# Four cross-attention layers on one core: the leftover keys' score products placed singly among the key groups of a sweep

## The reference, cut to what matters

```python
qh = (q @ Wq + bq).reshape(B, Lq, H, D).transpose(0, 2, 1, 3)
kh = (k @ Wk + bk).reshape(B, k.shape[1], H, D).transpose(0, 2, 1, 3)
vh = (v @ Wv + bv).reshape(B, v.shape[1], H, D).transpose(0, 2, 1, 3)
att = jnp.einsum('bhqd,bhkd->bhqk', qh, kh) * scale
att = jax.nn.softmax(att, axis=-1)
y = jnp.einsum('bhqk,bhkd->bhqd', att, vh)
...
x = x + jnp.tanh(g_xattn[0]) * _L0_xattn_ref(_layernorm(x), ctx_1024, ctx_1024, ...)
x = x + jnp.tanh(g_ffn[0]) * _L0_ffn_ref(_layernorm(x), ...)
```

## Time and profile before

| | us |
|---|---|
| median of 3 runs (3147.51 to 3158.24) | 3156.18 |
| the profiled execution's own time | 3158.26 |
| span of its trace | 3156.5 |
| PE busy in the span | 3041.5 (96%) |
| ACT busy | 2547.7 (81%) |
| DVE busy | 438.2 (14%) |
| POOL busy | 196.5 (6%) |

### The profile page before, as it was taken

The page is one execution under the profiler, slowest core; times in us unless marked ns, Lnnn a source line. Parts: engine busy times, 40 slices in busy tenths (PEclk is TensorE's granted clock), DMA queues, the critical chain, the costliest instruction groups (busy, mean ns, idle before and its releaser), DMA issues.

```text
span 3156.5 us, 56669 instructions
## 1 busy us (share of the span) xinstructions
PE 3041.5 (96%) x18432; PEld 1131.8 (36%) x18432; DVE 438.2 (14%) x1290; ACT 2547.7 (81%) x2960; POOL 196.5 (6%) x715
## 2 busy tenths in 40 slices
PE   6799999999989989999999999899899999999999
PEld 3432222322233532322332323666522222322256
DVE  3600000100012420000110001644300000100012
ACT  3489999999963269999999998332299999999963
POOL 2000000000000000000000000200000000000000
PEclk9989999999989989999999999999999999999999
DMA  6811111111140011111111113110011111111110
GB/s 190 235 34 37 37 37 36 37 38 37 37 110 0 1 33 37 38 37 37 60 43 38 38 37 93 38 56 1 1 35 37 37 37 43 57 38 37 37 39 7
DMA packets 147561, 146.31 MB, mean 46 GB/s; under 512 B 17512, under 2 KB 100956, under 8 KB 147436
## 3 DMA queue, kind: packets, MB, share of 16 engines
q1 hardware_dynamic: 141552, 142.57, 14.6%
q10 hardware_dynamic: 5884, 2.08, 0.3%
HBM read 115.21 MB, written 29.57 MB: 46 GB/s over the span
## 4 chain that ended last, share of the span: by engine, by line
PE 92%; DVE 4%; issue 1%; SPq 1%; POOL 1%; ACT 1%; DMA 1%; ACTq 0%; DVEq 0%; POOLq 0%
PE PS L2124 39%; PE PS L2143 32%; PE PS L740 5%; PE PS L725 5%; PE PS L727 2%; PE PS L1036 2%; PE PS L1022 1%; SPq L1511 1%; PE PS L1961 0%; PE PS L1023 0%; PE PS L1071 0%; PE PS L1971 0%; PE PS L2038 0%; PE PS L2104 0%; PE PS L2110 0%
## 5 line engine op out<-in xcount | busy, mean ns | idle before, releaser
L1897 ACT ACTIVATE probs<-PS 128x1024 f32<-128x1024 f32 x2496 | 2276.3, 1417 | 26.0 <-PE PS L2143 22.3
L2124 PE MATMUL PS<-probs,vr 128*32 128x512 f32 (+1 forms) x9984 | 1328.3, 604 | 1.9 <-DVE accs L2363 1.9
L2143 PE MATMUL PS<-qs,kr 35*128 35x512 f32 (+2 forms) x4992 | 1109.0, 492 | 6.6 <-ACT probs L1897 3.5
L2143 PEld LDWEIGHTS PS<-qs,kr 35*128 35x128 f32 x4992 | 459.9, 184 | 1278.0 <-ACT probs L1897 1101.1
L763 ACT ACTIVATE probs<-PS 128x512 f32<-128x512 f32 x192 | 114.5, 597 | 272.4 <-PE PS L725 144.3
L1731 POOL COPY vr<-vs 128x72 f32 (+1 forms) x624 | 157.7, 253 | 2793.0 <-PE PS L2124 2453.4
L2124 PEld LDWEIGHTS PS<-probs,vr 128*32 128x32 f32 x9984 | 197.4, 108 | 321.7 <-issue 213.9
L2363 DVE COPY accs<-PS 128x512 f32<-128x512 f32 x12 | 8.3, 692 | 1301.2 <-PE PS L2110 1301.2
L740 PEld LDWEIGHTS PS<-wide,probs 128*128 128x128 f32 x1280 | 151.5, 194 | 17.5 <-issue 16.7
L740 PE MATMUL PS<-wide,probs 128*128 128x128 f32 x1280 | 153.8, 277 | 0.5 <-DVE kf L798 0.5
L2361 DVE TENSOR_TENSOR PS<-PS,stair 128x256 f32<-128x256 f32 x64 | 25.3, 430 | 659.5 <-PE PS L2143 659.5
(11 more groups left out here) (299 smaller groups left out, 1152.5 us busy)
## 6 DMA issues: line engine op xcount, KB each, us to landing
kr<-key_pieces SPq DMA_DIRECT2D x1248, 64.0 KB
key_pieces<-kparts SPq DMA_DIRECT2D x36, 288.0 KB, 4.5
kr<-mask_strips SPq DMA_DIRECT2D x624, 4.0 KB
key_pieces<-probs SPq DMA_DIRECT2D x32, 288.0 KB, 4.8
vs<-values SPq DMA_DIRECT2D x2, 3672.0 KB, 16.9
values<-v_next SPq DMA_DIRECT2D x9, 432.0 KB, 5.5
values<-probs SPq DMA_DIRECT2D x8, 432.0 KB, 5.2
accs<-in_ctx SPq DMA_DIRECT2D x12, 192.0 KB, 4.3
```

The source lines that it names most:

```text
L1897: sc.activation(prob[n % RING][:, :, q0:], PS[:, bank:bank + 2, q0:], ACT.Exp, scale=SCALE).then_inc(p_ready, 1)
L2124: last = te.matmul(PS[32 * j:32 * j + 32, 7, q0:], vr[s.buf(c)][:, at_v:at_v + 32], prob[(n + j // 2) % RING][:, j % 2, q0:], start=fresh, ...
L2143: last = te.matmul(o, kr[b][own, p, :], qs[own, T8 // 2 * s.hh + p, 512 * s.qh + q0:512 * s.qh + 512], start=True, stop=True)
```

## The change

The four score products of a sweep's leftover keys are no longer one block at the joint behind it. Each stands alone behind a `values` call: in the second to fourth sweep of an attention in chunks 1 and 2 of that same sweep, in the first sweep in chunks 48 and 49. The value product of the second to fourth sweep moves into chunk 48 of its own sweep; that of the first sweep stays at the joint behind it. On ScalarE `exps_left` of the second to fourth sweep comes after that sweep's third chunk. TensorE's early transposes get a wait for the third sweep's `left_done` (bank 6), and DVE's copy of the accumulator now waits for the sweep's last `values` (`pv_done`) beside `left_used`.

```diff
--- before.py
+++ after.py
@@ -399,6 +399,8 @@
 
             if pair == 0:
                 pe.wait_ge(acc_ev, NSW * a + 2 * h + 2)
+                if h == 0:
+                    pe.wait_ge(left_done, NSW * a + 3)
             elif h == 0:
                 pe.wait_ge(at_rd, NT * a + 2)
             for j in range(2):
@@ -1906,8 +1908,10 @@
                     for c in range(TC):
                         for p in range(4):
                             exps(c, p)
-                            if prev and (c, p) == (0, 1):
+                            if s.w % NSW == 1 and (c, p) == (0, 1):
                                 exps_left(prev)
+                    if prev:
+                        exps_left(s)
                     with act.Fori(1, EXP_ROUND) as i:
                         for c in range(TC):
                             for p in range(4):
@@ -1921,8 +1925,6 @@
                     for c in range(ROUNDS_S * TC, s.n):
                         for p in range(4):
                             exps(c, p, q0=s.seen(c))
-                    if s.w % NSW == NSW - 1:
-                        exps_left(s)
                 between_act(act, a)
 
 
@@ -2093,16 +2095,18 @@
                 pe.wait_ge(qc_act, QU // 2 * (a + 1))
                 pe.wait_ge(qc_dve, QU // 2 * (a + 1))
 
-                def left_scores(s):
-
-                    if s.w % NSW == 0:
-                        pe.wait_ge(left_in, LEFT_IN * (a + 1))
-                    if s.w:
-                        pe.wait_ge(left_done, s.w)
-                    for tt in range(T8 // 2):
-                        t8 = T8 // 2 * s.hh + tt
-                        last = te.matmul(PS[:, 6, :], k_left[:, P * t8:P * t8 + P], qs[:, t8, 512 * s.qh:512 * s.qh + 512], start=(tt == 0), stop=(tt == T8 // 2 - 1))
-                    last.then_inc(left_ready, 1)
+                def left_scores(s, tt):
+
+                    if tt == 0:
+                        if s.w % NSW == 0:
+                            pe.wait_ge(left_in, LEFT_IN * (a + 1))
+                        if s.w:
+                            pe.wait_ge(left_done, s.w)
+                    t8 = T8 // 2 * s.hh + tt
+                    last = te.matmul(PS[:, 6, :], k_left[:, P * t8:P * t8 + P], qs[:, t8, 512 * s.qh:512 * s.qh + 512],
+                                     start=(tt == 0), stop=True, skip_group_check=True)
+                    if tt == T8 // 2 - 1:
+                        last.then_inc(left_ready, 1)
 
                 def left_values(s):
 
@@ -2146,15 +2150,17 @@
                     scores(0, 0)
                     if prev:
                         values(prev, prev.n - 1, 0)
-                        left_scores(prev)
                     scores(0, 1)
                     if prev:
                         values(prev, prev.n - 1, 1)
-                        left_values(prev)
+                        if prev.w % NSW == 0:
+                            left_values(prev)
                     for c in range(1, TC):
                         for g in range(2):
                             scores(c, g)
                             values(s, c - 1, g)
+                            if prev:
+                                left_scores(s, 2 * (c - 1) + g)
                     if s.w % NSW == 2:
                         for i in range(1, ROUNDS_S):
                             for c in range(TC):
@@ -2172,11 +2178,13 @@
                         for g in range(2):
                             scores(c, g)
                             values(s, c - 1, g)
+                            if prev is None and c < ROUNDS_S * TC + 2:
+                                left_scores(s, 2 * (c - ROUNDS_S * TC) + g)
+                        if prev and c == ROUNDS_S * TC:
+                            left_values(s)
                     if s.w % NSW == NSW - 1:
-                        left_scores(s)
                         for g in range(2):
                             values(s, s.n - 1, g)
-                        left_values(s)
 
                 between_pe(pe, a)
 
@@ -2360,6 +2368,7 @@
                             dve.wait_ge(s_ready, n + 1)
                             v.tensor_tensor(diagonal, diagonal, stair[:, :].unsqueeze(1).to_broadcast([P, 2, P]), ALU.add).then_inc(s_cut, 1)
                     dve.wait_ge(left_used, s.w + 1)
+                    dve.wait_ge(pv_done, s.quads + 2 * s.n)
                     v.tensor_copy(accs[:, s.hh, 512 * s.qh:512 * s.qh + 512], PS[:, 7, :]).then_inc(acc_ev, 1)
                     if s.w == NSW + 2:
                         scale_dve(dve, 0)
```

## The result

The change makes the kernel **slower by 0.5%**: median 3174.64 us over 20 executions against 3156.72 over 20; ratio 1.0052, 95% interval 1.0034 to 1.0069. One execution of each is some 2,100 us longer than the others; it counts in these medians (without it they are 3173.99 and 3156.26) but not in the ratio nor in what follows, where 19 of the changed kernel lie from 3153.19 to 3183.43 and 19 of the kernel before from 3147.05 to 3161.11. The forecast was 3157.5 with 3146 to 3165 as range, so the time lies outside it.

What follows compares the result with a forecast made beforehand. ScalarE was taken to set a sweep's pace, TensorE having 0.17 us to spare per step. The terms -6.7 + 3.7 + 8.2 + 1.5 - 5.4 gave +1.3 us, a median of 3157.5, range 3146 to 3165.

Steps and rivals of the forecast that it cites:

- rival D: TensorE's clock falls to 1.2 GHz, exponentials take 1.33 us each for 48 steps of two: +40, 3197 us; chance 0.01.
- item 1: Old losses at the joints between sweeps go: 6 x 1.0 and, in the second attention, 3 x 0.2; -6.7 us.
- batch rule: Skill rule that matmuls should go back to back in batches; by it dealing the products out is the wrong direction.
- Item 2: Value product of sweeps 1 to 3 moves into chunk 48: 9 x 0.41, +3.7 us.
- The single product: A lone score product between `values` and scores pays both edges, its weights not loaded ahead: 0.43 us.
- drain: Skill rule that a change of tiling mode drains TensorE; it spoke against the change, with 36 more such changes.
- rival B: Single products cost a quarter of the block, 0.285 us, weights loaded behind `values`: -4.4, 3151.8 us; chance 0.2.
- C: A drain on both sides of single products costs more than the block's edges show; at 0.8 us each, 3171; chance 0.09.
- Item 3: ScalarE time lost to single products in the sweeps and behind the joints, all three attentions: +8.2 us.
- the cover: Delay of a step's scores that ScalarE absorbs without loss: 0.64 us taken, 0.55 by a second reading.
- Item 5: Attention ends come earlier, the block and value product no longer behind the last exponential: 2 x 1.73 + 1.95, -5.4 us.
- Rival A: Everything hides: cover over 1.05 us, singles nearly free, -10.6, 3145.6 us; chance 0.07.

Runs made afterwards that it cites:

- b2_fill: The whole change, plus four extra score products as a block at joints 1 to 2 and 2 to 3 of the second attention; median 3158.74 us.
- a1_again: The changed kernel run again, unaltered; median 3164.44 us, ratio to the kernel before 1.0026 to 1.0066.
- a2_block: The change, with each sweep's four score products as one block (chunk 1 of sweeps 1 to 3, chunk 48 of sweep 0); median 3160.37 us.
- a4_outer: The change in the first and third attention only, the second as before; median 3158.06 us, ratio 0.9998 to 1.0020.
- d4_midspin: The change in the second attention only, plus four extra full-height products in chunk 1 behind joints 1 to 2 and 2 to 3; median 3163.65 us.
- c3_one: The change in the second attention only, with four extra products at joint 1 to 2 and nothing at joint 2 to 3; median 3160.90 us.
- c1_wait: The change in first and third attention only, TensorE awaiting the accumulator copy before chunk 1's scores at joints 1 to 2 and 2 to 3; median 3157.61 us.

## Why the prediction was wrong

- **What failed is the weighing of rival D, and item 1 behind it.** D was set at 0.01 because "with early work dealt between steps from 545 to 615 the clock stayed at 1.00". That row answers another question. It shows that work added between steps does no harm, and b2_fill agrees; the clock falls from what item 1 took away. Item 1 priced the second attention's joints at 0.2 us each and booked them as a gain. The block and the value product cost nearly nothing there because TensorE had run ahead through the masked chunks, and for the same reason their removal leaves it idle. Measured: -0.6 booked; paid, beyond the steps' +2.4, some 15 us of the median in the first measurement and some 5 in the second (a1_again, 7.1 over the kernel before).
- **D's price.** It was +40 for 48 steps. The mechanism is another in place and size: two joints, up to 27.3 us each in the profiles, at about 0.4 us lost per us at 1.2 GHz (10.7 for 27.3, 14.0 for 34.1). From the earlier trace rows, 1.33 against 0.917, it would be 0.31; steps with a single take 3.74 there.
- **The batch rule** of the Trainium skill (Perfetto Trace Analysis, Matmul Optimizations), named beside D: its direction is borne out in part. a2_block has 3160.37 against 3164.44 on the same chip and none of twelve over 3165 against six, though the intervals of the two ratios meet at 1.0026; a4_outer deals out as many products per sweep and keeps its clock, and where the clock stays the block costs as much as the singles.
- **Item 2** (value product at chunk 48, 0.41): 0.42. **The single product**, 0.43: 0.42. The two-sided wait at the change of shape is as read from the block's edges, and the Trainium skill's drain (TensorEngine Tiling, Key Properties) agrees; rival B falls with the load at 546.46. **C** falls for the same reason.
- **Item 3**: joint 0 to 1 took 1.26 (1.3 forecast), joint 1 to 2 0.51 (0.4). The term was short by 0.1 per joint: the second single behind the joint is lost in full (0.26), where the cover was to take part of it.
- **Item 5**: 1.62, 1.95 and 1.62 against 1.73, 1.95 and 1.73. Items 3 and 5 make up most of the difference between +2.4 and +1.3. By the ledgers, without the falls the median would be about 3159 (an estimate: 3156.7 and 2.4), inside the range.
- **Rival A** (everything hides) falls with the measured lumps.
- **The range** could not hold the time, as it left out a clock rival whose only counter-evidence came from another attention and another kind of edit. (Its lower end, 3146, also leaves out the 3145.6 of rival A that it is said to reach from.)
- **Open**: what exactly brings the clock down behind the narrow chunks. Idle TensorE alone does not (joint 0 to 1); whether the missing full-height work does so alone, or only with idle, no run tells, as none takes it away without leaving TensorE idle. Open too: why a fall lasts 6.8 us once and 27.3 the next time where no block follows it. In the profiles the four falls with a block behind them (a2_block, d4_midspin) last 3.4 us and the six without 6.8 to 27.3, and no execution of these two runs is over 3167; that the singles prolong a fall is not shown.

## To carry to other kernels

Work that hides for nothing may still hold TensorE's clock: before moving it away, look at what TensorE does in that place without it, above all behind narrow or masked chunks, and not only at the time it frees. If a median moves and the profiled execution doesn't, sort the executions by mean granted clock and profile again until one with a low clock is in hand. Work that is needed anyway is better kept there than replaced: four extra products behind the fall kept it to 3.4 us at the second attention's joints, but d4_midspin is still 0.25% slower than the kernel before, and for the stretch at the start of an attention no gain is shown.

## What the runs showed of the hardware

- The clock falls to 1.2 GHz in a part of the executions only, at the same place of the same program: behind 0.59 us of idle TensorE in a1_again, not behind 0.80 in c3_one, not behind 0.85 with the value product at joint 0 to 1 in b2_fill, nor behind 0.88 among full-width steps in c1_wait.
- TensorE was busy without a pause for the 27.3 us at 1.2 GHz in a1_again before 2.4 came back, although it was then what ScalarE waited for.
- More work can be faster: b2_fill, with eight extra products, has a median of 3158.74 (ratio to before 1.0003) where the same kernel without them has 3164.44 and 3174.64 (1.0046 and 1.0052) in its two measurements.
- A single full-height product between 32-column and 35-row ones costs 0.42 us at 2.4 GHz and 0.73 at 1.2 GHz (3.74 less 3.01), against 0.285 in a block at 2.4 GHz (1.14 for four).
